# Weights of the second routed layer's first eight slots loaded at the end of the softmax layer

## What is computed

```
x = x + L0_attn(layernorm(x))   # causal linear attention, gate, then a soft mixture of 4 experts
x = x + L0_ffn(layernorm(x))    # each token goes to one of 8 experts (128 -> 256 -> 128)
x = x + L1_attn(layernorm(x))   # softmax attention within each sequence
x = x + L1_ffn(layernorm(x))    # argmax over 8 scores, one expert a token:
                                # y = gelu(x w1[e] + b1[e]) w2[e] + b2[e], 128 -> 512 -> 128
```

## Time and profile before

| what | value |
|---|---|
| median of 3 runs | 1366.82 us |
| range of the runs | 1359.93 to 1367.71 us |
| profiled execution, own time | 1369.93 us |
| its span, first to last instruction | 1368.1 us |
| granted TensorE clock, mean | 0.933 |
| TensorE matmul busy | 1215.5 us (89%) |
| softmax layer's last barrier | about 1208 us of the span |
| second routed layer | from there to the end, some 160 us |

### The profile page before, as it was taken

The page is one execution under the profiler, slowest core; times in us unless marked ns, Lnnn a source line. Parts: engine busy times, 40 slices in busy tenths (PEclk is TensorE's granted clock), DMA queues, the critical chain, the costliest instruction groups (busy, mean ns, idle before and its releaser), DMA issues. The chain is left out here.

```text
span 1368.1 us, 32567 instructions
## 1 busy us (share of the span) xinstructions
PE 1215.5 (89%) x9954; PEld 953.4 (70%) x9954; DVE 993.8 (73%) x3299; ACT 817.5 (60%) x1699; POOL 775.2 (57%) x938
## 2 busy tenths in 40 slices
PE   3899999999996899999999995599499999759998
PEld 1566666776765777777777773498277777549997
DVE  4698989999844789999999998388478887612222
ACT  2354545455426788888888883366277777525553
POOL 3477777777640344554554555144658887526666
PEclk8999999999857999999999997699699999869999
DMA  2333122212132313212122120686121222188771
GB/s 100 96 100 100 58 79 65 83 54 80 56 80 66 62 40 67 42 46 69 39 50 66 41 72 27 165 257 202 43 83 63 68 63 54 60 308 292 265 262 60
DMA packets 81673, 132.75 MB, mean 97 GB/s; under 512 B 14674, under 2 KB 41819, under 8 KB 81584
## 3 DMA queue, kind: packets, MB, share of 16 engines
q1 hardware_dynamic: 56912, 90.17, 23.0%
q0 software_dynamic: 9792, 21.52, 5.1%
q10 hardware_dynamic: 14880, 19.99, 5.1%
HBM read 94.34 MB, written 29.81 MB: 91 GB/s over the span
## 5 line engine op out<-in xcount | busy, mean ns | idle before, releaser
L1280 DVE TENSOR_TENSOR m_Sl<-m_S,m_Sh 128x512 fp32r<-128x512 f32 x256 | 205.6, 813 | 38.6 <-ACT m_S L1202 37.1
L1197 ACT ACTIVATE m_Sh<-PS,W 128x512 fp32r<-128x512 f32 x256 | 177.2, 692 | 59.7 <-PE PS L1120 42.3
L1202 ACT ACTIVATE m_S<-PS,W 128x512 f32<-128x512 f32 x256 | 175.7, 686 | 8.0 <-DVE m_Sl L1280 8.0
L1581 POOL DMA_INDIRECT rows<-r_row,r_posi x128 | 136.2, 1064 | 34.5 <-issue 32.8
L850 DVE TENSOR_TENSOR am<-PS,C 128x512 f32<-128x512 f32 x192 | 119.6, 679 | 27.8 <-PE PS L478 27.2
L1118 PE MATMUL PS<-m_HH,m_w1h 128*128 128x512 f32 x256 | 107.2, 419 | 17.7 <-ACT m_S L1202 11.1
L1835 PEld LDWEIGHTS PS<-f_wt,f_hid 128*128 128x128 f32 x936 | 117.2, 193 | 4.6 <-ACT f_hid L1880 0.4
L1824 PE MATMUL PS<-f_xT,f_wt 128*128 128x256 f32 x468 | 118.5, 390 | 0.1
L1835 PE MATMUL PS<-f_wt,f_hid 128*128 128x128 f32 x936 | 117.7, 276 | 0.2 <-ACT f_hid L1880 0.2
L1135 PE MATMUL PS<-m_Sl,m_w2h 128*128 128x512 f32 x256 | 102.6, 401 | 1.3 <-DVE m_Sl L1280 0.7
L1132 PE MATMUL PS<-m_Sh,m_w2h 128*128 128x512 f32 x256 | 101.8, 397 | 1.5 <-DVE m_oe L1266 1.5
(11 more groups left out here) (252 smaller groups left out, 3037.7 us busy)
## 6 DMA issues: line engine op xcount, KB each, us to landing
f_wt<-wr SPq DMA_DIRECT2D x39, 578.0 KB, 4.5
f_row<-rows SPq DMA_DIRECT2D x39, 260.0 KB, 2.9
m_gb<-gates SPq DMA_DIRECT2D x8, 1024.0 KB, 8.1
m_raw<-gates SPq DMA_DIRECT2D x8, 1024.0 KB, 8.2
sb<-z_rows ACTq DMA_DIRECT2D x15, 512.0 KB, 5.7
f_row<-rows SPq DMA_DIRECT2D x39, 132.0 KB, 3.2
f_wt<-wr SPq DMA_DIRECT2D x20, 256.0 KB, 3.2
f_wt<-wr ACTq DMA_DIRECT2D x19, 256.0 KB, 4.0
```

The costliest lines, as they stand in the source:

```text
L1197: nc.scalar.activation(Sh[:, n % 4, :], PS[:, n % 3, :], ACT.Silu, bias=w("b1")[:, n:n + 1]).then_inc(sh_ready, 1)
L1202: nc.scalar.activation(S[:, n % 3, :], PS[:, n % 3, :], ACT.Silu, bias=w("b1")[:, n:n + 1]).then_inc(s_ready, 1)
L1280: nc.vector.tensor_tensor(Sl[:, n % 4, :], S[:, n % 3, :], Sh[:, n % 4, :].bitcast(F32), ALU.subtract).then_inc(sl_ready, 1)
L1581: nc.gpsimd.indirect_dma_start(out=self.rows, out_offset=bass.IndirectOffsetOnAxis(ap=self.posi[:, u, t:t + 1], axis=0), in_=self.row[:, u ...
```

## The change

The buffer for the second routed layer's weights and its eight semaphores are made ahead of softmax_attention. There SyncE, once its four paddings are issued, waits for the table of slots and issues the weight loads of slots 0 to 7 (a register load and a DMA of 128 x 4,624 bytes each); only behind them does it wait for all paddings. In routed(1), `load` leaves the weights out for slots 0 to 7 and does both loads from slot 8 on. For the first routed layer the wait for the paddings is a call of its own at the same place as before.

```diff
@@ program @@
-            routed(0, sems=sems, rows=rows_dram[0], weights=wr0, dest=mid_dram, stored=stored[0], **slots, **shared)
-            softmax_attention(sems=sems, mid=mid_dram, rows=rows_dram[1], scattered=scattered[1], **slots, **shared)
-            routed(1, sems=sems, rows=rows_dram[1], weights=wr1, dest=out, stored=stored[1], **slots, **shared)
+            routed(0, wt=None, weights_in=None, sems=sems, rows=rows_dram[0], weights=wr0, dest=mid_dram, stored=stored[0], **slots, **shared)
+            wt1 = ctx.enter_context(nc.sbuf_tensor("wt1", [P, DEPTH, wr1.shape[2]], F32))
+            wt1_in = [sems.enter_context(nc.semaphore(f"wt1_in{u}")) for u in range(DEPTH)]
+            softmax_attention(sems=sems, mid=mid_dram, rows=rows_dram[1], scattered=scattered[1], weights=wr1, wt=wt1, weights_in=wt1_in,
+                              **slots, **shared)
+            routed(1, wt=wt1, weights_in=wt1_in, sems=sems, rows=rows_dram[1], weights=wr1, dest=out, stored=stored[1], **slots, **shared)
@@ Routing.pad: its last wait becomes a method, called where pad's callers end @@
+    def all_padded(self, eng):
         eng.wait_ge(self.padded, 16 * (SPARE // SLOT + EXPERTS))
@@ mixture, block.sync and block.scalar @@
             routing.sp_padding(sp)
+            routing.all_padded(sp)
...
             routing.pad(act, range(EXPERTS // 2, EXPERTS))
+            routing.all_padded(act)
@@ routed @@
-        wt = sb("wt", [P, DEPTH, weights.shape[2]])
+        if not layer:
+            wt = sb("wt", [P, DEPTH, weights.shape[2]])
...
-        weights_in = [sem(f"weights_in{u}") for u in range(DEPTH)]
+        if not layer:
+            weights_in = [sem(f"weights_in{u}") for u in range(DEPTH)]
@@ routed, block.sync, load(s, u) @@
-                with_weights = layer == 1 or s % 2 == 0
+                with_weights = since(s, DEPTH) if layer else s % 2 == 0
@@ softmax_attention, block.sync @@
             routing.sp_padding(sp)
+            sp.wait_ge(routing.table, 12)
+            for u in range(DEPTH):
+                e = sp.value_load(slot_expert[0:1, u:u + 1], min_val=0, max_val=EXPERTS - 1)
+                sp.dma_start(wt[:, u, :], weights[bass.ds(e, 1), :, :].rearrange("o p n -> (o p) n")).then_inc(weights_in[u], 16)
+            routing.all_padded(sp)
```

More of the change, by code:

```diff
@@ L1682, in pad, with routed @@
                           self.padding[:, :, :]).then_inc(self.padded, 16)
+    def all_padded(self, eng):
         eng.wait_ge(self.padded, 16 * (SPARE // SLOT + EXPERTS))
-def routed(layer, nc, sems, X, w, c, PS, before, ones, minus_half, eps, scratch, rows, weights, dest, slot_row, slot_expert, where, stored):
+def routed(layer, wt, weights_in, nc, sems, X, w, c, PS, before, ones, minus_half, eps, scratch, rows, weights, dest, slot_row, slot_expert, where, stored):
     chunks = (2, 4)[layer]
@@ L1983, in _, with softmax_attention @@
                 close(NSLOT - 1, LAST, TURNS - 1)
-def softmax_attention(nc, sems, X, w, c, PS, before, ones, minus_half, eps, scratch, mid, rows, slot_row, slot_expert, where, scattered):
+def softmax_attention(weights, wt, weights_in, nc, sems, X, w, c, PS, before, ones, minus_half, eps, scratch, mid, rows, slot_row, slot_expert, where, scattered):
     with ExitStack() as ctx:
```

## The result

| | before | changed |
|---|---|---|
| median | 1366.41 us (16 runs, 1359.72 to 1371.42) | 1373.16 us (16 runs, 1366.37 to 1381.40) |
| profiled execution, span | 1368.1 us | 1371.2 us |

The ratio of the times is 1.0046, with a 95% interval of 1.0028 to 1.0065: the changed kernel is slower by 6.3 us (3.8 to 8.9), half a per cent. The forecast was 1372.0 us, 5.2 us slower.

A forecast was written before the change was run, and what follows sets the result against it. TensorE bounds the kernel, so its start after the seam counts: rows behind 4.73 MB of weights put the first up product at 1220.3 instead of 1215.11 us; 1366.82 + 5.2 = 1372.0 us, range 1365 to 1378.

The forecast's parts named there:

- The bound (TensorE's start hangs on the second rows): Seam before the second routed layer: slot 1's transposes precede the first up product, which starts 0.49 us after them.
- The gain of 1.2 to 1.6 us from what is removed: Routed layer on SP: eight weight DMAs and register loads fewer, so rows of slots 0 and 1 are issued sooner.
- The added issue on SP, 10.0 us: Behind SP's fourth padding: eight pairs of register load and DMA, three at 1.52 and five at 1.09 us.
- The bytes on the engines, 12.2 us on top of the paddings: DMA engines in the seam: 4.73 MB of weights at 389 GB/s, through at 1218.4 us.
- Total work is additive: DMA engines: paddings until 1206.2 plus 12.2 us of weights give 1218.4 us, whatever their order.
- The landing of the rows behind them, 0.68 us each: Rows of slots 0 and 1, 0.27 MB each, land behind the weights at about 1219.1 and 1219.8 us.
- Waiting behind the queue: SP's queue: rows wait for the 4.73 MB ahead of them; rival A, the forecast, +5.2 us, chance 0.62.
- Rival B: Barrier itself late, as paddings or scatters are starved by SP's weights: +9.0 us, 1375.8 us, chance 0.17.
- Rival C: Rows don't wait behind the weights and land in 2.7 and 2.9 us: +2.3 us, 1369.1 us, chance 0.12.
- Rival D: Not slower: SP's eight pairs fit into its 6.0 us of waiting at 0.75 us each; 1365.2 us, chance 0.05.

The follow-up runs named there:

- the run without bytes: Changed kernel with its eight early weight DMAs cut to 16 bytes a partition and the weights loaded in the routed layer as before; ratio 1.0039 (1.0014 to 1.0064).
- fixed experts: Changed kernel with its eight early weight DMAs from fixed experts 0 to 7, without register loads; ratio 1.0047 (1.0025 to 1.0070).
- the last two kernels: Changed kernel without early loads, slots 0 and 1 issued ahead of the barrier: 1.0021, 1.0003; also slot 0's weights behind the paddings: 0.9995, 0.9985.

## Why the prediction was right

**The bound (TensorE's start hangs on the second rows): right.** Every run's first up product follows the transposes of slot 1, and behind it the kernel is the same to 2 us (152.6 to 154.7).

**The gain of 1.2 to 1.6 us from what is removed: right in kind.** With one early load a part of it shows, 0.9 to 1.4 us by seam; with eight it is hidden.

**The added issue on SP, 10.0 us: 10.7.** Three slow pairs and five fast ones, as reasoned, the slow ones at 1.75 us instead of 1.52. Rows of slot 0 were issued at +16.9 instead of +16.1. That alone cost 4.5 to 5 us in the run without bytes, and is hidden under the transfers in the changed kernel, as forecast.

**The bytes on the engines, 12.2 us on top of the paddings: right.** The weights were forecast to be through at 1218.4 - 1196.76 = +21.6 us, and by the bytes of SP's queue they were at about +21.5. "Total work is additive" held in the sum, though not at 389 GB/s throughout: beside the paddings the full engines gave 254 GB/s for two us, and with the weights alone 411, and the two made up for each other. That is luck in part: with fixed experts the mixed stretch was slower (249 and 201 GB/s), and by the same count the weights were through at +22.8.

**The landing of the rows behind them, 0.68 us each: too small, and this is the term that was off.** Rows of slots 0 and 1 were forecast to land at +22.3 and +23.0 us. The first transposes waited for slot 0 until +24.0, and slot 1 landed at +24.6, 2.5 and 3.1 us behind the weights instead of 0.7 and 1.4. The forecast let a transfer land when the sum of bytes reaches it, but the bytes of more than four row transfers had moved when the second landed. Whether the 16 engines were unevenly far on or the landing itself takes this long, no run separates. So the sum gave 5.2 us where the profiles show 6.9 (7.4 against the second profile of before) and the ratio of the times 6.3.

**Waiting behind the queue: the time was right, the reason was not.** I took the order of SP's queue as the cause. On ScalarE's empty queue the rows waited as long. By what the runs show, it is enough that the engines are full with what was issued before. Either reason puts the rows behind the 4.7 MB, so the time came out by luck as far as the reason goes.

**Rival B, a late barrier by starved paddings or scatters: not in the changed kernel, a little in others.** There they were through at +10.7 and +11.5 us, and SP's issue opened the barrier. But the paddings ended at +12.3 with two early loads, +12.0 with four and +13.1 with fixed experts, instead of +10.9: weights beside the paddings put them off by 1.1 to 2.2 us there, more than the 0.7 us by which two profiles of before differ. The Trainium skill ("DMA: Bandwidth & Descriptors", section "Queues, rings and completion order") has the engines alternate between queue rows by packets. In the changed kernel the last paddings lost nothing by it (5.7 and 6.1 us against 5.1 and 6.3). With faster issue ScalarE's took 2.1 us longer, and the rows on ScalarE's queue got no packet for 3.5 us. So this rule would have let me expect the quick landing that the run didn't show: the measurement decides, and no simple alternation explains it.

**Rival C, no waiting: no**, 6.6 us of landing for the rows of slot 1. **Rival D, hidden issue: no**, a pair took 1.1 to 1.75 us, not 0.75.

## What to carry to other kernels

An idle stretch of an engine queue isn't idle transfer capacity: before work is put ahead of a barrier, count its bytes against the DMA share of that stretch, and ask what the first instructions behind the barrier need. Anything issued early that isn't needed first delays what is; here the first slot's weights fit in and the eight slots' didn't. Where a gain is 2 us in a kernel whose front moves by more than 10, compare the stretch from a fixed event in the trace, and say that the whole time doesn't show it.

## What the runs showed of the hardware that I had not expected

Reads of weights and writes of 1 KB paddings together moved 201 to 254 GB/s at a DMA share of 1.0 to 1.1, where paddings and scatters alone move 315 (before, 1200 to 1206 us) and weights alone 411 to 419. A transfer on a queue of its own waited 3.5 us for its first packet while another queue's earlier transfers filled the engines, instead of 1.0, and took 7.0 us in all instead of 2.7. A register load on SP took 0.9 us instead of 0.27 while paddings were in flight. On one occasion (the kernel without early loads, and one run each of the last two kernels) the softmax layer took 272 to 275 us instead of 233, in kernels that don't differ there, and its wait list has a row that the other profiles don't have:

```profile
ACT s_probT L2229 <- remote: 28.4, 7, 6.2
```

In that row of the kernel without early loads, seven waits of up to 6.2 us are put down to something outside the core. What it was stays open; those kernels' times were compared with runs of before on the same occasion, which were as long (median 1403.98 us).
